# Row maxima of attention scores by plain free-axis max, with the causal mask added in PSUM by an accumulating identity matmul

## The reference, cut to what matters

```python
qkv = x @ W_qkv.T; q, k, v = split into 16 heads of 16
scores = einsum('bhqd,bhkd->bhqk', q, k) / 4
scores = where(tril, scores, -inf)
attn = softmax(scores)
y = layernorm(x + (attn @ v) @ W_proj.T)
out = layernorm(y + (silu(y @ Wg.T) * (y @ Wu.T)) @ Wd.T)
```

## Time and profile before

| what | us |
|---|---|
| median of 3 runs | 1554.58 |
| the 3 runs | 1554.26, 1554.58, 1557.93 |
| span of the profiled execution, first to last instruction | 1558.1 |
| PE busy in it | 1467.7 |
| DVE busy | 1208.7 |
| ACT busy | 940.5 |
| POOL busy | 353.7 |

### The profile page before, as it was taken

The page is one execution under the profiler, slowest core; times in us unless marked ns, Lnnn a source line. Parts: engine busy times, 40 slices in busy tenths (PEclk is TensorE's granted clock), DMA queues, the critical chain, the costliest instruction groups (busy, mean ns, idle before and its releaser), DMA issues.

```text
span 1558.1 us, 34187 instructions
## 1 busy us (share of the span) xinstructions
PE 1467.7 (94%) x9300; PEld 689.1 (44%) x9300; DVE 1208.7 (78%) x3122; ACT 940.5 (60%) x2055; POOL 353.7 (23%) x436
## 2 busy tenths in 40 slices
PE   8999969999998998998998998999898999999997
PEld 5665523333333333333333333333333666666664
DVE  4555577897897987987997987998762777887776
ACT  3545415776776775776776776777576444444443
POOL 5000001211211221221121121122121443444434
PEclk9999967999998999999999999999899999999999
DMA  7777993575475466457447547546401022212211
GB/s 246 229 238 229 232 138 42 72 86 67 62 90 73 56 83 85 57 74 90 61 66 91 67 57 92 71 61 110 65 13 38 28 81 81 69 52 81 81 55 41
DMA packets 173313, 140.58 MB, mean 90 GB/s; under 512 B 80208, under 2 KB 148304, under 8 KB 173136
## 3 DMA queue, kind: packets, MB, share of 16 engines
q1 hardware_dynamic: 173136, 138.46, 48.7%
HBM read 87.29 MB, written 50.33 MB: 88 GB/s over the span
## 4 chain that ended last, share of the span: by engine, by line
PE 83%; issue 6%; DVE 6%; DMA 3%; ACT 2%; SPq 0%; DVEq 0%; POOL 0%; POOLq 0%; ACTq 0%
PE ps L1180 18%; PE ps L1109 15%; PE ps L1092 14%; PE ps L1238 11%; PE ps L1055 7%; PE ps L1253 4%; PE ps L1151 4%; PE ps L1062 4%; DVE ps L841 3%; PE ps L1199 3%; DMA q_stack<-max_rows 1%; DVE row_max L841 1%; PE ps L1223 1%; PE ps L1044 1%; ACT x_hi_rows L738 1%
## 5 line engine op out<-in xcount | busy, mean ns | idle before, releaser
L841 DVE CUSTOM_DVE_ANT_0 ps<-ps,causal 128x1024 f32<-128x1024 f32 (+7 forms) x1024 | 746.1, 790 | 129.1 <-PE ps L1092 125.1
L700 ACT ACTIVATE probs<-ps 128x512 f32<-128x512 f32 (+3 forms) x1536 | 653.7, 495 | 274.4 <-PE ps L1109 265.6
L1109 PE MATMUL ps<-q_stack,k_stack 99*128 99x512 bf16 (+3 forms) x1536 | 402.7, 334 | 39.2 <-issue 19.5
L1092 PE MATMUL ps<-k_stack,q_stack 96*128 96x512 bf16 (+3 forms) x1536 | 361.8, 338 | 13.4 <-DVE row_max L841 5.9
L589 POOL TENSOR_SCALAR_AFFINE_SELECT probs<-probs 128x512 f32<-128x512 f32 x256 | 162.5, 635 | 806.8 <-ACT probs L700 806.8
L1180 PE MATMUL ps<-probs,v_ones 128*32 128x512 f32 (+3 forms) x3072 | 335.3, 509 | 0.5 <-POOL probs L589 0.5
L1109 PEld LDWEIGHTS ps<-q_stack,k_stack 99*128 99x128 bf16 x1536 | 132.8, 98 | 266.5 <-ACT probs L700 143.5
L1092 PEld LDWEIGHTS ps<-k_stack,q_stack 96*128 96x128 bf16 x1536 | 135.1, 99 | 187.5 <-DVE row_max L841 51.4
L619 POOL TENSOR_TENSOR h_lo<-h_sb,h_hi 128x512 f16<-128x512 f32 x96 | 119.3, 1248 | 197.9 <-ACT h_hi L757 197.9
L841 DVE DVE_READ_ACCUMULATOR2_ANT row_max<- 128x1 f32 x1024 | 145.9, 142 | 0.0
L749 ACT ACTIVATE silu<-ps 128x512 f32<-128x512 f32 x96 | 57.3, 597 | 127.5 <-PE ps L1238 127.5
(11 more groups left out here) (89 smaller groups left out, 1272.8 us busy)
## 6 DMA issues: line engine op xcount, KB each, us to landing
qk_parts<-parts SPq DMA_DIRECT2D x64, 384.0 KB, 2.8
q_stack<-qk_parts SPq DMA_DIRECT2D x192, 128.0 KB, 6.9
k_stack<-qk_parts SPq DMA_DIRECT2D x192, 128.0 KB, 7.3
x_sb<-in_L_attn_x SPq DMA_DIRECT2D x32, 512.0 KB, 4.5
v_rows<-v_sb SPq DMA_DIRECT2D x16, 512.0 KB, 3.2
v_flat<-v_rows SPq DMA_DIRECT2D x32, 256.0 KB, 10.8
attn_rows<-attn_sb SPq DMA_DIRECT2D x64, 128.0 KB, 2.1
v_sb<-attn_rows SPq DMA_DIRECT2D x16, 512.0 KB, 5.5
```

What stands on the lines that cost most here:

```text
L700: act.activation(probs[s % RING][:, j, 0:w], ps[:, 4 + n % 3, 0:w], ACT.Exp, scale=SOFT_SCALE).then_inc(exp_done, 1)
L841: last = dve.tensor_tensor_reduce(scores, scores, causal[:, T - w:T], 1.0, LOWEST, ALU.add, ALU.max, row_max[:, j * QT + qt:j * QT + qt + 1])
L1092: last = pe.matmul(ps[:, 2 * pair + c0 // CH, c0 % CH:c0 % CH + w], q_stack[g][0:ROWS, j, tile_cols(qt)], k_stack[g][0:ROWS, j, k0:k0 + w] ...
L1109: pe.matmul(ps[:, 4 + n % 3, 0:w * P], k_stack[g][0:ROWS_M, j, tile_cols(kt)], q_stack[g][0:ROWS_M, j, q0:q0 + w * P], start=True, stop=Tr ...
```

## The change

The units are cut in another way. A query tile of 5 to 8 blocks (qt 4 to 7) is a unit by itself, at the start of its pair of banks. A query tile of 1 to 4 blocks (qt 0 to 3) is done for two heads in one unit, each head in a bank of its own. So each group has 24 units in place of 18, with 2 to 8 blocks in place of always 8; the blocks are 144 as before, and so are the score matmuls, 48. The last 128 columns of each query tile get a second matmul, which adds the mask: the identity `ident_bf` as weights, the 128 x 128 bf16 tile `above` (the lowest value above the diagonal, 0 elsewhere) as moving operand, accumulated on the scores. There is one for each query tile, 32 in a group and 1024 in all. DVE then takes the maximum by one plain `tensor_reduce` for a unit, with two results where the unit holds two heads, and writes nothing back to PSUM. `UNITS_AHEAD` goes from 12 to 16 (of 24), and 40 units come before the loop. The planner's constant for DVE's fixed part goes from 68 ns for a query tile to 150 ns for a unit, and its count of PE columns includes the mask matmuls. The mask tile on POOL is [128, 128] bf16 instead of [128, 1024] f32.

```diff
-    COLS, EXP, ROW_MAX, PV, TURN = 54, (50, 107), (68, 134), (110, 214), 428
+    COLS, EXP, ROW_MAX, PV, TURN = 54, (50, 107), (150, 134), (110, 214), 428
...
-                cols = sum(qt + 1 for _, qt in unit_items[m % nu])
-                pe += cols * COLS
-                dve = max(dve, pe + PE_DVE) + len(unit_items[m % nu]) * ROW_MAX[0] + cols * ROW_MAX[1]
+                rows, qt = unit_items[m % nu]
+                cols = len(rows) * (qt + 1)
+                pe += (cols + len(rows)) * COLS
+                dve = max(dve, pe + PE_DVE) + ROW_MAX[0] + cols * ROW_MAX[1]
...
-        for k in (j, j + 1):
-            max_units += [[(k, QT - 1)]] + [[(k, QT - 1 - t), (k, t - 1)] for t in range(1, QT // 2)]
-        max_units.append([(j, QT // 2 - 1), (j + 1, QT // 2 - 1)])
+        for qt in range(QT - 1, QT // 2 - 1, -1):
+            max_units += [((j,), qt), ((j + 1,), qt), ((j, j + 1), QT - 1 - qt)]
...
-    UNITS_AHEAD = 12
+    UNITS_AHEAD = 16
...
-                for j, qt in max_units[u % NU]:
-                    w = (qt + 1) * P
-                    scores = ps[:, 2 * pair:2 * pair + 2, :].rearrange("p a b -> p (a b)")[:, k0:k0 + w]
-                    last = dve.tensor_tensor_reduce(scores, scores, causal[:, T - w:T], 1.0, LOWEST, ALU.add, ALU.max,
-                                                    row_max[:, j * QT + qt:j * QT + qt + 1])
-                    k0 += w
-                last.then_inc(s_free, 1)
+                rows, qt = max_units[u % NU]
+                w = (qt + 1) * P
+                by_tile = row_max[:].rearrange("p (j t) -> p j t", j=HG)
+                if len(rows) == 1:
+                    scores = ps[:, 2 * pair:2 * pair + 2, :].rearrange("p a b -> p (a b)")[:, 0:w]
+                    dve.tensor_reduce(by_tile[:, rows[0], qt:qt + 1], scores, AX.X, ALU.max).then_inc(s_free, 1)
+                else:
+                    dve.tensor_reduce(by_tile[:, rows[0]:rows[0] + 2, qt], ps[:, 2 * pair:2 * pair + 2, 0:w], AX.X,
+                                      ALU.max).then_inc(s_free, 1)
...
-                for j, qt in max_units[u % NU]:
-                    k0, k_end = 0, (qt + 1) * P
-                    while k0 < k_end:
-                        w = min(CH - c0 % CH, k_end - k0)
-                        last = pe.matmul(ps[:, 2 * pair + c0 // CH, c0 % CH:c0 % CH + w],
-                                         q_stack[g][0:ROWS, j, tile_cols(qt)], k_stack[g][0:ROWS, j, k0:k0 + w],
-                                         start=True, stop=True)
-                        k0, c0 = k0 + w, c0 + w
+                rows, qt = max_units[u % NU]
+                for r, j in enumerate(rows):
+                    for k0 in range(0, (qt + 1) * P, CH):
+                        bank, w = 2 * pair + r + k0 // CH, min(CH, (qt + 1) * P - k0)
+                        held = k0 <= qt * P < k0 + w
+                        last = pe.matmul(ps[:, bank, 0:w], q_stack[g][0:ROWS, j, tile_cols(qt)],
+                                         k_stack[g][0:ROWS, j, k0:k0 + w], start=True, stop=not held)
+                        if held:
+                            last = pe.matmul(ps[:, bank, w - P:w], ident_bf[:], above[:], start=False, stop=True)
```

More of the change, by code:

```diff
@@ L33 @@
 ACT = mybir.ActivationFunctionType
+AX = mybir.AxisListType
 RING = 3
 def attention_steps(slots, diagonal, unit_items, ahead, units_from, units_to, has_next):
-    COLS, EXP, ROW_MAX, PV, TURN = 54, (50, 107), (68, 134), (110, 214), 428
+    COLS, EXP, ROW_MAX, PV, TURN = 54, (50, 107), (150, 134), (110, 214), 428
     MASK, COPY, COPY_ROWS, NORMALISE, SPLIT = 594, 478, 158, 650, 950
@@ L208, in block_kernel @@
         ident_f16 = sb("ident_f16", [P, P], F16)
-        causal = sb("causal", [P, T], F32)
+        above = sb("above", [P, P], BF16)
         minus_half = sb("minus_half", [P, TILES], F32)
@@ L547, in _ @@
                                pattern=[[-1, P]], channel_multiplier=1).then_inc(consts_ready, 1)
-            pool.memset(causal[:], 0.0).then_inc(consts_ready, 1)
+            pool.memset(above[:], 0.0).then_inc(consts_ready, 1)
             pool.memset(minus_half[:], -0.5)
             pool.wait_ge(consts_ready, 3)
-            pool.affine_select(out=causal[:, T - P:T], in_=causal[:, T - P:T], compare_op=ALU.is_ge, fill=LOWEST,
+            pool.affine_select(out=above[:], in_=above[:], compare_op=ALU.is_ge, fill=LOWEST,
                                base=0, pattern=[[-1, P]], channel_multiplier=1).then_inc(consts_ready, 1)
@@ L836, in row_maxima @@
                 dve.sem_inc(dve_passed, 1)
-                k0 = 0
-                for j, qt in max_units[u % NU]:
-                    w = (qt + 1) * P
-                    scores = ps[:, 2 * pair:2 * pair + 2, :].rearrange("p a b -> p (a b)")[:, k0:k0 + w]
-                    last = dve.tensor_tensor_reduce(scores, scores, causal[:, T - w:T], 1.0, LOWEST, ALU.add, ALU.max,
-                                                    row_max[:, j * QT + qt:j * QT + qt + 1])
-                    k0 += w
-                last.then_inc(s_free, 1)
+                rows, qt = max_units[u % NU]
[7 more added lines that the diff above has]
+                                      ALU.max).then_inc(s_free, 1)
             def split_max(count, uses, first=False):
@@ L1078, in _ @@
             pe.wait_ge(preset, 6)
+            pe.wait_ge(consts_ready, 6)
             pe.sem_inc(pv_done, RING)
@@ L1086, in scores_for_max @@
                 pe.wait_ge(s_free, use + 1)
-                c0 = 0
-                for j, qt in max_units[u % NU]:
-                    k0, k_end = 0, (qt + 1) * P
-                    while k0 < k_end:
-                        w = min(CH - c0 % CH, k_end - k0)
-                        last = pe.matmul(ps[:, 2 * pair + c0 // CH, c0 % CH:c0 % CH + w],
-                                         q_stack[g][0:ROWS, j, tile_cols(qt)], k_stack[g][0:ROWS, j, k0:k0 + w],
-                                         start=True, stop=True)
-                        k0, c0 = k0 + w, c0 + w
+                rows, qt = max_units[u % NU]
[7 more added lines that the diff above has]
+                            last = pe.matmul(ps[:, bank, w - P:w], ident_bf[:], above[:], start=False, stop=True)
                 last.then_inc(s_ready, 1)
```

## The result

The change makes the kernel slower: 1610.13 us, median of 4 runs (1602.89 to 1611.77), against 1555.62 us, ratio 1.0347 with a 95% interval of 1.032 to 1.0373. The forecast was 1597 in a range of 1578 to 1626. Direction and mechanism hold; of 54.5 us the forecast had 42.4.

The account below looks back on a forecast made before the run. PE was taken as the bound: a steady group of 28.37 us, plus 1.78 for mask matmuls, minus 0.45 of absorbed waits, gives 29.7. Over 30.3 groups, with +2 for low clock, that is +42, so 1597; range 1578 to 1626.

Parts of the forecast that it names:

- PE is the bound: Attention's steady group: PE is full, with true waits of about 0.9 us of 28.37, so added PE work costs time.
- DVE sets the pace: Rival in attention: groups follow DVE, 1.0 us less each, 1524; if waits just cancel, 1555. Chance 0.05 faster, 0.04 no change.
- The price of a mask matmul: On PE, 128 columns cost 55 to 56 ns each, 1.78 us a group, 54 us for 971 on the path.
- the load in the open: Rival on PE: its weight load paces each mask matmul, 98 ns, 1638 us; chance 0.07 together with the accumulation rival.
- the turn-around of the accumulation: Rival on PE: each mask matmul waits for the write before it, 217 ns, 1754 us; chance 0.07 with the load rival.
- DVE's relief: On DVE, the fixed part is paid 24 times in place of 32, making a group 1.0 us lighter.
- The waits: PE's waits in a group: added work absorbs half of about 0.9 us, 0.45 us a group, 14 us in all.
- new waits: Six more units a group could each wait 0.09 us, 0.5 us a group; more than that had chance 0.03.
- 27.5 us for a group's steps: Sum of PE's steps in a steady group, leaving true waits of about 0.9 us of 28.37.
- changes from bf16 to f32: On PE in a group, a bf16 step before an f32 step takes 0.09 us longer; 14 such changes, 1.2 us.
- the lower clock at the loop's turns: Some six mask matmuls in each of seven loop turns cost double at the low clock, +2 us.
- The start-up: Stage ahead of the loop: 0.2 us more on the path against 0.4 us less, called even.

Follow-up runs that it names:

- run 9: Kernel after, with DVE reducing only the first half of each unit's columns, PE and order unchanged: 1607.03 us, ratio 1.0336 to the kernel before.
- run 10: Kernel before, its cut and order, with plain unmasked reduces over only the first half of each query tile's columns: 1545.77 us, ratio 0.994.
- run 4: Kernel after, with one extra reduce of 8 columns on DVE ahead of each unit: 1607.38 us, ratio 1.0354 to the kernel before.
- run 1: Kernel before, with only the mask matmuls added over a tile of zeros, DVE still adding the mask itself: 1595.90 us, ratio 1.0266.
- run 8: Kernel after, with two mask matmuls for each query tile, each adding half of the lowest value: 1653.59 us, ratio 1.0633 to the kernel before.
- run 5: The change with the 18 units and order of the kernel before: real mask by mask matmuls, a plain reduce for each query tile: 1586.68 us, ratio 1.0214.
- run 2: Kernel before, its units and order, with plain reduces on DVE and no mask in the maxima: 1546.29 us, ratio 0.9952.
- run 3: Kernel after, its units and order, without the mask matmuls, so the maxima are unmasked: 1572.75 us, ratio 1.0123 to the kernel before.
- run 12: Kernel after, with DVE reducing half the columns, and the last value slot and ACT's output copy two score tiles earlier: 1600.42 us, ratio 1.0308 to the kernel before.
- run 11: Kernel after, with a group's last value slot and ACT's output copy moved two score tiles earlier: 1601.77 us, ratio 1.0303 to the kernel before.
- run 6: Kernel after in another order, by the planner's two constants for the maxima on DVE, (40, 133) for (150, 134): 1599.54 us, ratio 1.0289 to the kernel before.
- run 7: Kernel before with plain unmasked reduces, in an order replanned with DVE cost 75 ns, score-tile lead 0.015 and 14 units ahead: 1553.73 us, ratio 1.0002.

## Why the prediction was right or wrong

**PE is the bound: right.** Four runs change DVE's work and leave PE's and the order alone. Half the columns (runs 9 and 10) are worth 0 us on the kernel after and 0.33 on the kernel before, the plain maxima 0.25, and 1.6 us more work (run 4) costs nothing. Two runs add only PE work, and three quarters or more of it come out as time in a steady group (1.50 and 1.43 us of 1.87; runs 1 and 8). The rival "DVE sets the pace" is dead. Of the two measures for PE that the Trainium skill names beside each other, matmul work done against the peak and weight-load time ("Perfetto Trace Analysis", "Identifying the Most-Contended Engine"), the second does not find this bound: by it PE is loaded for 12.99 of 30.38 us, 43%. The first is not worked out here.

**The price of a mask matmul: too low by 5 to 8%.** I took 55.5 ns, it is 58 to 60. That is 0.1 us a group and 3 us in all. The rivals of the load in the open (98 ns) and the turn-around of the accumulation (217 ns) are out. The Trainium skill's 81 ns for a stream of weight load and matmul pairs ("TensorE: Matmul & The Clock Gate", "Back-to-back issue gap") is not what this stream shows. Its formula for a single matmul, 128 columns at 2.4 GHz and 2.5 ns, gives 55.8 ns, an estimate that fits the score matmuls' 55; the mask matmuls lie 2 to 4 ns above it.

**DVE's relief: right.** It was 1.0 us a group by forecast and is 1.3 in busy time. The rate of the reduce was taken from the right row; its fixed part was taken too high (0.13 us, measured 0.08).

**The waits: this is the term that was mis-sized.** "I take half absorbed, 0.45 us a group": with the old cut and order that and more happens. Mask matmuls there cost 1.50 us for 1.87 of columns, the DVE relief brings 0.25, and so 0.6 us of waits go (run 5). Against it the forecast had new waits only as an upper end, 0.5 us a group. They came, and are larger: the new cut and its order cost 0.75 to 0.85 us in a steady group and 1.1 to 1.2 in the one ahead of the loop's turn. By the sum of the prediction, 27.5 us for a group's steps and 1.87 for its masks, the waits are 1.0 us after, where they were 0.9; I had expected 0.45. That the measured time still lies in the range is in part luck: its upper end had no absorbed waits and 0.5 us of new ones, and what came is more of both. The sum holds small slips as well: a group has 13 changes from bf16 to f32, not 14, and the 2 us for the lower clock at the loop's turns do not show, as these groups grew less than the steady ones. In time, relative to the kernel before: plain maxima -7.5 (run 2), mask matmuls +41 (run 5 over run 2), new cut and order +21 (after over run 5), together 54.

**Where the new waits stand.** The starts of the matmuls in the traces give it. What a matmul takes beyond its columns (215, 161, 108 and 55 ns for 512 to 128 columns, 59 for a mask matmul, 0.09 us more ahead of an f32 step), where it is over 15 ns, in us a group:

| group | behind score tiles | at the turn |
|---|---|---|
| before | 0.49 | 0.34 |
| run 2 | 0.45 | 0.18 |
| run 3 | 0.84 | 0.61 |
| run 5 | 0.19 | 0.06 |
| after | 0.48 | 0.49 |
| after, ahead of the loop's turn | 0.75 | 0.75 |
| run 12, ahead of the loop's turn | 0.75 | 0.22 |

The bf16 columns with the masks add up to the same 18.58 us in run 5 and in the kernel after. So the 0.75 us between them are waits and not dearer work: 0.43 at the turn and 0.29 behind score tiles, where the profile names ACT's exponentials. Both are larger again in the group ahead of the loop's turn.

**What holds PE at the turn.** Shown: one place, before the turn, where the last units are small. PE runs out of work there while ACT's copy of the output is on its way, and 0.23 us go when the copy is moved (run 11), 0.16 more when DVE is out of the way too (run 12). In the group ahead of the loop's turn the two together give 0.49. Run 6 shows that another order of the same instructions saves 0.23 us at a steady group. So the order, not the number of units or handshakes, carries at least that part. What stays open is the cause of the 0.29 us behind score tiles: no run took these waits for ACT apart, and a cut cannot be changed without its order. What makes the two places worse in the group ahead of the loop's turn was not tried either.

**How I read the wait before the turn.** The prediction put 0.34 us there to DVE, as the profile did. For the kernel before that was about right: DVE out of the way gives 0.25 to 0.33 us. For the kernel after the same reading failed in my ninth expectation, since the profile names the releaser that PE met, and a second one stood 0.2 us behind it.

**The start-up: not shown to be wrong.** I called it even. In the two profiled executions the rows of maxima came 3.9 us sooner after the change, PE was back at 2.4 GHz 14 us sooner, and the second mT came 6.6 us sooner. But the trace of before is the latest of fourteen there, and with the 252.5 to 256.7 us of the four kernels with its units and order about 1 us is left, an estimate. The sum of attention alone was 40 + 2 forecast and 56.3 measured, and this is near the 54.5 between the medians, as it has to be if the start-up is about even.

**A faster kernel.** Run 2 beats both, by a little: 0.9952 (0.9932 to 0.9971); the same edit in another order gives 1.0002 (run 7). It leaves the mask out of the maxima, so a row subtracts the maximum of a few more scores than it uses. That cancels in the normalisation, as long as no masked score exceeds the row's own by so much that all its exponentials vanish. With the mask kept by matmul, no version tried reaches the kernel before.

## What to carry to other kernels

Before work is moved from one engine to another, sum up the receiving engine's starts over one period: if the sum leaves 0.9 us of 28, every instruction that it gets is paid in full but for the waits that it fills, here 80% of the mask matmuls' columns. Count as a cost of its own that the steps are cut and ordered anew; try the parts of a change in the old order first. And if the profile names a wait's releaser, look for what would have released it next: here 9 of DVE's 24.4 us of work could go without moving the end of a wait in a steady group.

## What the runs showed of the hardware that I had not expected

- An accumulating matmul of 128 columns with 128 rows of identity weights takes 58 to 60 ns from start to start directly behind the score matmul that it adds to, against 55 for a plain one of 96 or 99 rows. A second one behind it takes 55 again (run 8), so neither its 128 rows nor the accumulation as such is the reason.
- A bf16 matmul ahead of the f32 values matmuls took 0.09 us longer (149 ns for a mask matmul), but ahead of the f32 turn, where nothing was waited for, the mask matmul took 60 ns (run 11). So this surcharge does not come with every change to f32.
- A reduce of 8 columns from PSUM added only 1.6 us / 24 = 67 ns to DVE's busy time when it stood ahead of another reduce.
- The group in which the loop turns took between 32.8 and 39.2 us over the kernels tried, at steady groups of 28 to 32. This spread is as large as some effects here, so the steady group was the better measure.
- The time at which PE gets the first rows of maxima lay between 230.3 and 236.4 us over the fourteen traces, one of each kernel, and did not follow the work ahead of it: the latest is that of the kernel before, while run 1 adds work and has 232.9. One trace on each side cannot tell a gain of some us there from this spread.
